# Cross attention in a decoder layer: maximum products only between score pieces; rope, splits, reciprocals and normalising in other chunks

## The reference, cut to what matters

```
kv_r = rope(kv_c)                                 # 1444 x 64 for each item
q_r, k_r = q_big @ W_qr, kv_r @ W_kr              # 16 heads, R = 64
scores = einsum('bhsr,bhlr->bhsl', q_r, k_r)      # 1600 query rows x 1444 per item
attn = softmax(scores, axis=-1)
ctx_c = einsum('bhsl,bld->bhsd', attn, kv_r)
x = x + einsum('bhsd,hkd->bhsk', ctx_c, w_kc_kv) @ Wo.T      # with the reshapes
```

## Time and profile before

| | before |
|---|---|
| runs | 2817.58, 2818.99, 2822.96 us, median 2818.99 |
| the profiled execution | span 2817.1 us, from first to last instruction; its own time stands nowhere apart from the three above, of which the lowest lies 0.5 over the span |
| instructions | 40800 |
| TensorE busy | 94% |
| VectorE, GpSimd, ScalarE busy | 72%, 54%, 36% |
| mean granted TensorE clock | 0.971 |
| rate of transfers | 31 GB/s |

### The profile page before, as it was taken

The page is one execution under the profiler, slowest core; times in us unless marked ns, Lnnn a source line. Parts: engine busy times, 40 slices in busy tenths (PEclk is TensorE's granted clock), DMA queues, the critical chain, the costliest instruction groups (busy, mean ns, idle before and its releaser), DMA issues. The chain is left out here.

```text
span 2817.1 us, 40800 instructions
## 1 busy us (share of the span) xinstructions
PE 2649.9 (94%) x13650; PEld 1632.3 (58%) x13650; DVE 2034.9 (72%) x3271; ACT 1026.2 (36%) x1537; POOL 1512.6 (54%) x438
## 2 busy tenths in 40 slices
PE   6999769999979999999999999999999999999598
PEld 4545457767635555555555555555555555555388
DVE  6888758888776777677767776777677767775475
ACT  3223221111114444444444444444444444444143
POOL 1544500000026776777677767776777677767421
PEclk9999879999969999999999999999999999999799
DMA  4000031212111001100010011001100010000011
GB/s 120 19 17 23 12 107 43 47 41 47 40 41 32 21 20 25 35 20 20 25 35 20 20 25 35 20 20 25 35 20 20 25 35 20 20 20 6 25 41 41
DMA packets 56196, 88.97 MB, mean 32 GB/s; under 512 B 7146, under 2 KB 47166, under 8 KB 56016
## 3 DMA queue, kind: packets, MB, share of 16 engines
q1 hardware_dynamic: 56144, 88.29, 12.3%
HBM read 65.13 MB, written 23.14 MB: 31 GB/s over the span
## 5 line engine op out<-in xcount | busy, mean ns | idle before, releaser
L1376 POOL TENSOR_TENSOR x_acc<-x_acc,x_prob 120x1600 f32<-120x1600 f32 (+1 forms) x320 | 1157.1, 3616 | 281.7 <-ACT x_prob L1392 277.9
L1485 DVE TENSOR_REDUCE x_mx<-x_ring 124x1 f32<-124x480 f32 (+3 forms) x1248 | 784.4, 658 | 424.6 <-PE x_ring L1595 424.0
L1392 ACT ACTIVATE x_prob<-x_scores 120x800 f32<-120x800 f32 (+1 forms) x768 | 633.1, 839 | 920.2 <-PE x_scores L1542 913.4
L1554 PE MATMUL x_context<-x_prob,x_kv 120*64 120x400 f32 (+1 forms) x3072 | 653.5, 519 | 0.0
L1539 PE MATMUL x_scores<-x_qa,x_ka 128*120 128x400 f32 (+1 forms) x1536 | 552.3, 360 | 0.0
L1542 PE MATMUL x_scores<-x_qb,x_kb 128*120 128x400 f32 (+1 forms) x1536 | 530.7, 345 | 0.0
L1595 PE MATMUL x_ring<-x_ka,x_qa 128*124 128x480 f32 (+3 forms) x1248 | 516.7, 437 | 3.2 <-DVE x_mx L1485 1.1
L1595 PEld LDWEIGHTS x_ring<-x_ka,x_qa 128*124 128x124 f32 (+1 forms) x1248 | 220.0, 186 | 321.7 <-issue 161.2
L1539 PEld LDWEIGHTS x_scores<-x_qa,x_ka 128*120 128x120 f32 (+1 forms) x1536 | 280.0, 182 | 107.4 <-issue 60.6
L1554 PEld LDWEIGHTS x_context<-x_prob,x_kv 120*64 120x64 f32 (+1 forms) x3072 | 166.8, 135 | 227.0 <-issue 162.7
L1542 PEld LDWEIGHTS x_scores<-x_qb,x_kb 128*120 128x120 f32 (+1 forms) x1536 | 280.0, 182 | 26.4 <-DMA x_qb<-scratch_m 0.2
(11 more groups left out here) (165 smaller groups left out, 2867.8 us busy)
## 6 DMA issues: line engine op xcount, KB each, us to landing
x_qraw<-scratch_qp SPq DMA_DIRECT2D x64, 400.0 KB, 5.2
scratch_qp<-q_qs SPq DMA_DIRECT2D x32, 400.0 KB, 3.8
x_raw<-in_ctx SPq DMA_DIRECT2D x32, 360.0 KB
a_x<-in_x SPq DMA_DIRECT2D x8, 400.0 KB
scratch_x<-a_x SPq DMA_DIRECT2D x8, 400.0 KB
q_x<-scratch_x SPq DMA_DIRECT2D x8, 400.0 KB
x_xr<-scratch_x SPq DMA_DIRECT2D x32, 100.0 KB
scratch_x<-x_x SPq DMA_DIRECT2D x32, 100.0 KB
```

Source lines behind the costliest of these rows:

```text
L1376: pool.tensor_tensor(acc[0:rows, parity], first, prob[0:rows, c % PR], ALU.add).then_inc(acc_done.sem, 1)
L1392: act.activation(prob[0:rows, c % PR, u * HALF:(u + 1) * HALF].rearrange("p (j s) -> p j s", j=2), psc[0:rows, u, :, 0:BANK], ACT.Exp).the ...
L1485: dve.tensor_reduce(mx[0:block_rows(r), r, i:i + 1], ring[0:block_rows(r), bank, 0:b - a], AX.X, ALU.max).then_inc(rg.read[bank], 1)
L1554: mm = pe.matmul(pav[DC * s:DC * s + DC, j, 0:BANK], kv[0:rows, parity, c], prob[0:rows, c % PR, cols], start=c == 0, stop=c == LC - 1)
```

## The change

The table `side` is written anew. `kvT` 0 and 1 move to chunk 0 and `kvT` 2 to chunk 1; `out` goes from between the context pieces of chunk 0 to behind the last score piece of chunk 1; the two `den` go from chunk 10 to the ends of chunks 4 and 5. The 39 maxima were spread evenly over all pieces of chunks 3 to 9, a context piece counting twice. They now stand behind score pieces only, six in each of chunks 2, 3 and 4, four in each of 5 to 8, five in 9.

VectorE's `rope` of the item after next is issued in chunk 11 of the slot before, between the two products of `normalise`. Slot n starts with the low part (`split_kv`) and `split_q`. ScalarE copies the denominators out of `ring` into a new tile `dens` (`save_den`, after the exponentials of chunks 4 and 5), VectorE inverts them in halves of 200 columns at the ends of chunks 5 to 8 (`invert`), and `normalise` is only the product, once in chunk 10 and once in chunk 11. ScalarE's high part of `ks` stands ahead of the slot's first exponentials, and `copy_turned` one half chunk after another from the first on.

The diff, with the lines of the tables and the parts that move:

```diff
-        for place, u in (((1, 3), ("kvT", 0)), ((2, 0), ("kvT", 1)), ((2, 3), ("kvT", 2)), ((C_M, 2), ("mT",)),
-                         ((C_M, 3), ("den", 0)), ((C_M, 5), ("den", 1)), ((0, 4), ("out",))):
+        for place, u in (((0, 1), ("kvT", 0)), ((0, 3), ("kvT", 1)), ((1, 1), ("kvT", 2)), ((1, 3), ("out",)),
+                         ((C_M, 2), ("mT",)), ((4, 5), ("den", 0)), ((5, 5), ("den", 1))):
...
-        ticks = [(c, i) for c in range(3, C_M) for i in range(PIECES) for _ in range(1 + (ORDER[i][0] == "context"))]
+        for c, at_pieces in ((2, (0, 1, 1, 2, 3, 3)), (3, (0, 1, 1, 2, 3, 3)), (4, (0, 1, 1, 2, 3, 3)), (5, (0, 1, 2, 3)),
...
+            def save_den(n, j):
+
+                wait(act, ctx_normed.sem, ctx_normed.at(n - 1, j + 1))
+                bank, value = rg.place(n, ("den", j))
+                act.wait_ge(rg.filled[bank], value)
+                act.copy(dens[:, j], ring[:, bank, 0:BANK]).then_inc(rg.read[bank], 1)
...
             def slot(n, parity, more):
+                if more:
+                    act.wait_ge(kv_roped.sem, kv_roped.at(n, 1))
+                    bank, value = rg.place(n - 1, ("kvT", 2))
+                    wait(act, rg.filled[bank], value)
+                    act.copy(ks[:, :, 0:DC].bitcast(F32R), rotated[:]).then_inc(kv_high.sem, 1)
...
-                        if 2 * c + u in (3, 4, 5) and more:
-                            copy_turned(n, 1 - parity, 2 * c + u - 3)
...
+                        if 2 * c + u in (0, 1, 2) and more:
+                            copy_turned(n, 1 - parity, 2 * c + u)
+                        if (c, u) in ((4, 1), (5, 1)):
+                            save_den(n, c - 4)
...
+            def invert(n, j, half):
+
+                bank, value = rg.place(n, ("den", j))
+                dve.wait_ge(rg.read[bank], value)
+                cols = slice(half * (BANK // 2), (half + 1) * (BANK // 2))
+                dve.reciprocal(rden[:, j, cols], dens[:, j, cols]).then_inc(rden_ready.sem, 1)
...
-                dve.reciprocal(rden[:, j], ring[:, bank, 0:BANK]).then_inc(rg.read[bank], 1)
...
                     if c == 0 and more:
-                        rope(n, 1 - parity)
+                        split_kv(n)
                         split_q(n, 1 - parity)
...
+                    if c in (5, 6, 7, 8):
+                        invert(n, (c - 5) // 2, (c - 5) % 2)
...
+                    if c == LC - 1 and ahead:
+                        rope(n + 1, parity)
+                    if c >= LC - 2:
+                        normalise(n, c - (LC - 2))
```

More of the change, by code:

```diff
@@ L1201, in phase_cross_attention @@
         ctxs = sb("ctxs", [P, 2, BANK])
+        dens = sb("dens", [P, 2, BANK])
         rden = sb("rden", [P, 2, BANK])
@@ L1248, in phase_cross_attention @@
         max_ready = sig("maxima_ready", 1, 1)
+        rden_ready = sig("denominators_inverted", 4, 4)
         ctx_normed = sig("context_normed", 2, 2)
@@ L1417, in slot @@
                             exponentials(n, c, u)
-                        if 2 * c + u in (3, 4, 5) and more:
-                            copy_turned(n, 1 - parity, 2 * c + u - 3)
-                    if c == 0 and more:
-                        act.wait_ge(kv_roped.sem, kv_roped.at(n, 1))
-                        bank, value = rg.place(n - 1, ("kvT", 2))
-                        wait(act, rg.filled[bank], value)
-                        act.copy(ks[:, :, 0:DC].bitcast(F32R), rotated[:]).then_inc(kv_high.sem, 1)
+                        if 2 * c + u in (0, 1, 2) and more:
+                            copy_turned(n, 1 - parity, 2 * c + u)
+                        if (c, u) in ((4, 1), (5, 1)):
+                            save_den(n, c - 4)
                     if c == 1 and more:
@@ L1430, in _ @@
             save_context(B)
+            for j in range(2):
+                save_den(B, j)
         @block.vector
@@ L1446, in rope, with split_kv @@
                 dve.tensor_tensor(rotated[:], t1[:], t2[:], ALU.add).then_inc(kv_roped.sem, 1)
+            def split_kv(n):
                 dve.wait_ge(kv_high.sem, kv_high.at(n, 1))
@@ L1458, in split_q @@
                                   ALU.subtract).then_inc(q_low.sem, 1)
+            def invert(n, j, half):
[3 more added lines that the diff above has]
+                dve.reciprocal(rden[:, j, cols], dens[:, j, cols]).then_inc(rden_ready.sem, 1)
             def normalise(n, j):
-                bank, value = rg.place(n, ("den", j))
+                wait(dve, ctx_saved.sem, ctx_saved.at(n, 0))
+                dve.wait_ge(rden_ready.sem, rden_ready.at(n, 2 * j + 2))
+                bank, value = rg.place(n, ("out",))
                 dve.wait_ge(rg.filled[bank], value)
-                if j == 0:
-                    wait(dve, ctx_saved.sem, ctx_saved.at(n, 0))
-                dve.reciprocal(rden[:, j], ring[:, bank, 0:BANK]).then_inc(rg.read[bank], 1)
-                dve.wait_ge(rg.read[bank], value)
-                before, value = rg.place(n, ("out",))
-                dve.wait_ge(rg.filled[before], value)
                 dve.tensor_tensor(ctxn[:, j], ctxs[:, j], rden[:, j], ALU.mult).then_inc(ctx_normed.sem, 1)
@@ L1486, in maximum, with slot @@
                                   ALU.max).then_inc(rg.read[bank], 1)
-            def slot(n, parity, more):
+            def slot(n, parity, more, ahead):
                 for c in range(LC):
                     if c == 0 and more:
-                        rope(n, 1 - parity)
+                        split_kv(n)
                         split_q(n, 1 - parity)
                     for u in beside[c]:
-                        if u[0] == "den":
-                            normalise(n, u[1])
-                        elif u[0] == "out":
+                        if u[0] == "out":
                             output(n, parity)
@@ L1513, in _ @@
             dve.wait_ge(memset.sem, N_MEMSET)
-            in_turn(dve, slot)
+            rope(-1, 0)
+            slot(-1, 1, True, True)
+            slot(0, 0, True, True)
+            with dve.Fori(0, (B - 4) // 2) as i:
+                for parity in (1, 0):
+                    slot(i * 2 + (2 - parity), parity, True, True)
+            slot(B - 3, 1, True, True)
+            slot(B - 2, 0, True, False)
+            slot(B - 1, 1, False, False)
             output(B, 0)
             for j in range(2):
+                for half in range(2):
+                    invert(B, j, half)
                 normalise(B, j)
```

7 lines of the change are left out of this document (5 added, 2 removed).

## The result

| | before | after |
|---|---|---|
| median of the runs | 2818.56 us (2817.58 to 2822.96) | 3077.44 us (3075.82 to 3080.14) |
| ratio | 1 | 1.092 [1.090, 1.093] |
| span of the profiled execution | 2817.1 us | 3074.0 us |
| mean granted TensorE clock | 0.971 | 0.939 |

A forecast was written before the change was run, and what follows sets the result against it. TensorE, busy 94%, was taken as the bound. Stall 8.1 plus clock 1.8 less gain 0.6 made 9.3 us at 30 slot ends, 279 us on a 2817.1 us span; with 1.9 for the median, 3097 us forecast, range 2955 to 3150.

The forecast's parts named there:

- stall at the transposes: Chunk 0: TensorE's first transpose waits for the low part, delayed by GpSimd's additions; 8.1 us a slot.
- half clock after it: After the stall TensorE runs 3.6 us at half speed: 1.8 us lost a slot, bounds 0 and 3.0.
- gain of the rest of the table: Uncut context steps and a removed transpose wait save 3.4 us a slot, denser maxima cost 2.8: gain 0.6.
- first and last slot: Both ends of the run shift by a microsecond or so either way: counted as nothing.
- The walk through VectorE's list: From the start of chunk 10, normalising products, rope and low part alternate with three GpSimd additions; low part done at T+15.3.
- a port kept through operations without a wait between them: Chunks 10 and 11: VectorE runs normalising and three rope operations unbroken to T+5.2; stall 7.3 us instead of 8.1.
- the port changing hands at every instruction: VectorE's products of two SBUF operands and GpSimd's additions take turns, each excluding the other for a whole instruction: 8.1 us stall.
- The first rival: At the slot end VectorE keeps the port through rope: stall of 4.0 us a slot, 2975 us; chance 15%.
- The second rival: Rope in chunk 11 is not held: gain of 0.6 us times 31 slots, 2800 us; chance 6%.
- The reciprocals: Halved, some 1.4 us each, they run while TensorE does a context step and makes no maxima: cost nothing.
- The third rival: Reciprocals reading SBUF each wait for a 3.6 us GpSimd addition, delaying maxima: 446 us more, about 3545; chance 4%.

The follow-up runs named there:

- rope in the pause: Changed kernel, with rope and low part made a slot earlier in GpSimd's pause and GpSimd's first addition waiting for the low part: 2805.1 us, ratio 0.995.
- GpSimd's wait: Changed kernel, with GpSimd's addition of chunk 10 held until VectorE has made the next item's low part: 2831.51 us, ratio 1.0046.
- rope back: Changed kernel, with rope alone put back at the slot start, ahead of the low part: 3111.07 us, ratio 1.104.
- the third experiment: Changed kernel, with rope and low part made early in the slot before, where GpSimd pauses, its first addition waiting for the low part: 2805.1 us, ratio 0.995.

## Why the prediction was right

Each term of its sum has a measured value now.

| term, a slot | predicted | measured |
|---|---|---|
| stall at the transposes | 8.1 us | 7.5 (172.3 in the 23 of the stretch above) |
| half clock after it | 1.8 | 1.6 (below) |
| gain of the rest of the table | 0.6 | 0.56 (56.33 less 55.77, rope in the pause) |
| net | 9.3 | 8.6 |
| times 30 | 279 | 258 |
| first and last slot | 0 | -1 |

**The stall** is the term that was mis-sized, by 0.6 us. The walk through VectorE's list has the right order at each step, and the measured ends, counted from T = 1730.33, are up to 0.5 earlier: the first normalising product done at T+3.4 (predicted 3.44), the first rope product at T+7.65 (7.9), rope at T+12.9 (13.4), the low part at T+14.8 (15.3). The walk gave VectorE's two turns between the additions 0.44 and 0.85 us on top of three full additions; they took 0.9 together, so the third addition is over by T+11.06, not 11.5. The transposes start at T+14.85, and were wanted at T+7.39, not 7.3. The 7.5 us lie nearer to the 7.3 that the prediction gave for a port kept through operations without a wait between them, but that way is refuted: by it the first rope product would not have been held.

**The turns.** The forecast rested on the port changing hands at every instruction. VectorE's rows show it: the first rope product had waited while the second addition ran, then got in for its own time, and the next product waited out the third addition. The first rival, a port kept through rope, expected one hold of the port for the whole of rope and a stall of 4.0; two holds of rope, 4.36 and 4.37, refute it. The sink products are drawn together, so their row alone does not tell whether the port changed hands between the two; with the third addition over, there was nobody left to take it. The second rival, rope not held, falls with the same rows. The low part, which the prediction had free of holds, was.

The Trainium skill, page "SBUF — State Buffer", section "Who interferes with whom", calls the shared pair of ports an exclusive lock for a whole instruction; the trace agrees, with 4.36 us for a product of 0.94 beside an addition of 3.83.

**The clock.** Chunk 0 of the changed kernel takes 13.03 us; the same products take 3.98 with rope in the pause, at full clock (from the context step at 1730.29 to that at 1734.27), and 7.46 are the stall: 1.6 us is what clock and restart cost. 1.8 was taken from the first slot of the kernel before, after a stall of half the length. What is lost is half of the 2.9 us of work at the lower level, up to about 1748.1. The other 0.2 are most likely restart and no clock: with GpSimd's wait chunk 0, and with it the slot, is 0.94 longer than with rope in the pause, at full clock, for a stall of 0.73 on average (19.7 us in 27 waits between 1000 and 2500 us). The 1.6 is no constant: in the run with rope back, stalls of 8.0 us cost 1.6, 2.1 and 3.0. The prediction's bounds of 0 and 3.0 were needed, and that its 1.8 came so near is in part luck. What sets the moment at which the clock comes back, no run shows.

**The packing** comes out as forecast by errors of opposite sign, so its 0.6 is luck. Six maxima were put at 0.8 and cost 0.85, five at 0.4 and cost 0.48, four at nothing and cost 0.06 (4.08 against 4.02). Three of six, one of five and four of four make 3.3, not 2.8. The rest shows when the lengths of the 12 chunks, from score product to score product in TensorE's timelines between 1000 and 2500 us, are compared between the kernel before and rope in the pause. Their means, chunk 0 to 11, are 6.94, 3.57, 4.55, 4.98, 4.79, 4.66, 4.87, 4.71, 4.87, 4.56, 4.71 and 3.14 us before, and 3.98, 7.01, 5.32, 5.33, 6.00, 4.76, 4.08, 4.09, 4.09, 4.72, 3.25 and 3.15 with rope in the pause. The table has what stands above a bare chunk of 3.14 us:

| a slot | before | rope in the pause | gain |
|---|---|---|---|
| maxima and cut context steps | 11.4 | 11.9 | -0.4 |
| wait of the transpose in chunk 2 | 0.4 | 0 | 0.4 |
| output product | 3.8 | 3.45 | 0.35 |
| three groups of transposes | 1.4 | 1.25 | 0.15 |
| transpose of the maxima, two sums of denominators | 1.57 | 1.45 | 0.1 |

The 39 maxima at 0.22 are 8.6 of the first row, so the cuts cost 2.9 before, near the 3.0 of the prediction, and the crowding costs 3.3 after: the maxima's new places lose 0.4 where the prediction had them gain 0.2. In its place stand 0.6 us that the prediction put at nothing, with the sentence that the moved sums and the moved output product "keep their context neighbours and cost what they did". The output product stood between the halves of a context step and now stands ahead of a whole one; together with the cut it took 3.8 us, and now takes 3.45. No run moves it alone, so that the cut is the reason is likely and not shown.

**The reciprocals** cost nothing and were never held: 1404 ns is the longest of 136. Beside 124 of them an addition begins, and it keeps its 3.60 to 3.63 us; four begin while an addition runs and take 1345 to 1404 ns. The third rival falls.

**The first and last slot** were put at "a microsecond or so". They come to -1 together, but through larger shifts: the maxima of slot -1 end 4.6 us later, 3.2 of it the two sums of denominators (1.6 us each there) that now stand among them, and slot 0, which no longer begins with them, is 5.1 us shorter. The range and the sign held. The time was 19.6 us under the forecast. The span grew by 22 less than the 279 of the sum; the median lies 3.4 above the profiled span, where the prediction added 1.9, and takes 1.5 of that back. The last 1 is a slip of the prediction: its own terms, 2817.1 + 279 + 1.9, give 3098 and not 3097.

## What to carry to other kernels

An operation that costs 0.94 us in one place of a list can cost 4.36 in another: before moving a VectorE operation of two SBUF operands, look at what GpSimd does in the new place, and at how soon the result is wanted there; here the price was one addition for each of them, on the path of TensorE. Where GpSimd is off the critical path and has slack, as here, let it wait for VectorE's group on a semaphore: that one wait took 246 us out of the changed kernel, and it is worth 136 us even with rope in GpSimd's pause. And a gain from packing should be tried part by part, chunk by chunk: the 0.56 us a slot of this change was real, but the part meant to bring it, the maxima between score products, lost 0.4 until they lay further apart. With that and the hold gone the kernel takes 2774 us, 1.5% under the kernel before.

## What the runs showed that was not expected

- GpSimd gets its turn even between VectorE operations that stand back to back with no semaphore between them: in the changed kernel after the first normalising product (1.67 us) and after the first rope product (4.36). The forecast rested on it and had no row for it.
- A hold appears as duration of the instruction, with no idle time before it and under VectorE's busy share. VectorE's busy share (72% before, 71% after) tells nothing of the 6.8 us of holds in the two rope rows of each slot. Compare the mean of one instruction with its time elsewhere: the line of the cosine product has 940, 4360 and 4369 ns as lowest, median and highest.

```profile
L1456 DVE TENSOR_TENSOR x_t<-x_raw,x_cosk x32: 940/4360/4369, 782.9 to 2771.3; 121x768 f32<-121x768 f32 x32
```

- The cast of the queries, one SBUF operand only, is held too. In the third experiment it stands beside the last addition of a slot, in VectorE's timeline behind the two normalising products:

```profile
1727.09 5.57 DVE L1510 TENSOR_TENSOR x_ctxn<-x_ctxs,x_rden 128x400 f32<-128x400 f32 x2
1732.58 4.38 DVE L1492 CAST x_qa<-x_qraw 128x1600 fp32r<-128x1600 f32 x1
```

It takes 0.99 us elsewhere for 1600 columns, 0.6 ns a column, where a reciprocal of 200 columns takes 1.39 us and was never held. The Trainium skill, page "SBUF — State Buffer", section "Who interferes with whom", counts casts among the operations that can take both pairs of ports and so contend; this row agrees, 4.38 against 0.99.

- ScalarE's exponentials showed no hold in the changed kernel, though GpSimd adds beside more than half of them: all 768 take between 829 and 844 ns.
